# Eight images through masked double attention on one core: row maxima turned by DMA, projections of q and k made whole in every second batch

## What is computed

```
x = x + L(gn(x))                       # x: 8 x 512 x 32 x 32, gn: 32 groups
L(x):
    g    = relu(mean_hw(x) @ w1 + b1) @ w2 + b2
    m    = sigmoid(g) > 0.5            # a gate for each channel
    hyp  = logmap0(mhsa(expmap0(x * m), hdn weights))
    euc  = mhsa(x * (1 - m), eu weights)
    return hyp + euc
mhsa(t):                               # t: 1024 tokens x 512 channels, 8 heads of 64
    q, k, v = split(t @ w_qkv + b_qkv)
    attn = softmax(q @ k.T / sqrt(64)) # 1024 x 1024 for each head
    return (attn @ v) @ w_o + b_o
```

## Time and profile before

| | |
|---|---|
| median of 3 runs | 4022.97 us (4020.16 to 4023.03) |
| the profiled execution's own time | 4021.88 us |
| its span | 4020.2 us |
| TensorE busy | 3937.1 us (98%) |
| GpSimd busy | 2664.2 us (66%) |
| VectorE busy | 2345.5 us (58%) |
| ScalarE busy | 1928.7 us (48%) |

### The profile page before, as it was taken

The page is one execution under the profiler, slowest core; times in us unless marked ns, Lnnn a source line. Parts: engine busy times, 40 slices in busy tenths (PEclk is TensorE's granted clock), DMA queues, the critical chain, the costliest instruction groups (busy, mean ns, idle before and its releaser), DMA issues.

```text
span 4020.2 us, 57048 instructions
## 1 busy us (share of the span) xinstructions
PE 3937.1 (98%) x21664; PEld 2379.5 (59%) x21664; DVE 2345.5 (58%) x2553; ACT 1928.7 (48%) x3489; POOL 2664.2 (66%) x1303
## 2 busy tenths in 40 slices
PE   4999999999999999999999999999999999999998
PEld 3556566565655656556565665656556565565654
DVE  5464755647556475565746557465674656646455
ACT  4454534545345453555535545354553545535443
POOL 4584875838667486674857658675685756858468
PEclk9999999999999999999999999999999999999999
DMA  8212031121311213112141120411113121121101
GB/s 277 100 42 95 32 116 58 43 95 32 124 50 48 95 32 126 53 48 90 32 135 49 48 79 32 142 48 68 53 47 127 48 74 48 56 96 44 58 11 64
DMA packets 137548, 293.12 MB, mean 73 GB/s; under 512 B 16704, under 2 KB 28992, under 8 KB 127296
## 3 DMA queue, kind: packets, MB, share of 16 engines
q1 hardware_dynamic: 137280, 289.47, 21.2%
HBM read 239.09 MB, written 50.33 MB: 72 GB/s over the span
## 4 chain that ended last, share of the span: by engine, by line
PE 94%; DVE 2%; POOL 1%; DMA 1%; issue 1%; ACT 1%; SPq 0%; POOLq 0%; DVEq 0%; ACTq 0%
PE aux_ps L1310 32%; PE acc_ps L1422 23%; PE score_ps L1408 22%; PE aux_ps L1359 8%; PE score_ps L1310 4%; PE aux_ps L1432 3%; DVE mxp L1173 1%; PE aux_ps L1369 1%; POOL sums L673 1%; DMA w_split<-v_y 0%; DMA w_split<-w_o 0%; DMA xin<-in_x_dram 0%; PE aux_ps L1328 0%; PE aux_ps L1325 0%; POOL w_o L653 0%
## 5 line engine op out<-in xcount | busy, mean ns | idle before, releaser
L673 POOL TENSOR_TENSOR sums<-sums,probs 128x1024 f32<-128x1024 f32 x768 | 1835.4, 2390 | 736.9 <-ACT probs L850 682.6
L1173 DVE TENSOR_REDUCE mxp<-aux_ps 128x2 f32<-128x1024 f32 x1014 | 1241.7, 1225 | 1299.9 <-PE aux_ps L1359 1291.5
L850 ACT ACTIVATE probs<-score_ps 128x512 f32<-128x512 f32 x2048 | 1058.1, 602 | 658.7 <-PE score_ps L1408 648.0
L1422 PE MATMUL acc_ps<-probs,v_y 128*64 128x512 f32 x4096 | 991.9, 605 | 0.0
L1310 PE MATMUL aux_ps<-xs,w_qk 128*128 128x512 f32 x2976 | 804.7, 408 | 0.0
L1310 PEld LDWEIGHTS aux_ps<-xs,w_qk 128*128 128x128 f32 x2976 | 524.8, 188 | 374.3 <-issue 279.1
L673 POOL TENSOR_TENSOR sums<-probs 128x1024 f32<-128x1024 f32 x128 | 305.0, 2383 | 432.8 <-ACT probs L850 432.1
L1422 PEld LDWEIGHTS acc_ps<-probs,v_y 128*64 128x64 f32 x4096 | 248.2, 136 | 475.2 <-issue 245.2
L1359 PE MATMUL aux_ps<-k_hi,q_hi 64*128 64x512 f32 x2028 | 454.0, 443 | 18.7 <-DVE mxp L1173 16.1
L1235 DVE RECIPROCAL den<-den 128x256 f32<-128x256 f32 (+1 forms) x240 | 443.4, 1848 | 17.3 <-ACT den L861 17.3
L1408 PE MATMUL score_ps<-q_hi,k_hi 64*128 64x512 f32 x2048 | 407.9, 393 | 1.0 <-issue 1.0
(11 more groups left out here) (142 smaller groups left out, 3195.2 us busy)
## 6 DMA issues: line engine op xcount, KB each, us to landing
w_qk<-w_split SPq DMA_DIRECT2D x124, 512.0 KB, 4.2
xin<-in_x_dram SPq DMA_DIRECT2D x232, 256.0 KB, 3.3
w_o<-w_split SPq DMA_DIRECT2D x32, 1024.0 KB, 7.3
w_v<-w_split SPq DMA_DIRECT2D x30, 1024.0 KB, 5.9
v_y<-in_x_dram SPq DMA_DIRECT2D x72, 256.0 KB, 3.0
y<-v_y SPq DMA_DIRECT2D x64, 256.0 KB, 2.0
xin<-y SPq DMA_DIRECT2D x64, 256.0 KB, 2.9
out_dram<-v_y SPq DMA_DIRECT2D x64, 256.0 KB, 6.5
```

Of the source, the lines that this page charges most:

```text
L673: pool.tensor_tensor(sums[h][:, :], a, probs[:, g % SLOTS_P, :], ALU.add).then_inc(c_sum[h].sem, 1)
L850: act.activation(probs[:, n % SLOTS_P, token_half(u % 2)], score_ps[:, u % SCORE_BANKS, :], ACT.Exp, scale=SCALE).then_inc(c_exp.sem, 1)
L1173: dve.tensor_reduce(mxp[:, :, n, h], ps, AX.X, ALU.max).then_inc(c_free["D"].sem, 1)
L1422: last = nc.tensor.matmul(acc_ps[head(j), :], v_y[:, m, head(2 * p + j)], probs[:, n % SLOTS_P, token_half(j)], start=(m == 0), stop=(m == ...
```

## The change

Row maxima. `combine` runs twice for each pair, after slots 11 and 15, once for each half of the queries. SyncE stores each result to DRAM (1024 numbers of 4 bytes, one by one) and, once this has landed, loads it back as two rows into `q_max` (`load_neg`). The matmuls, the identity and the copies are gone. The score tile waits for the load at the first tile of each phase.

Projections. Each stands whole in one batch, which is always even. The denominators move from `b` = 4`ph` + 5 to 4`ph` + 6 (even), for the last phase but one to 28, and the reciprocal comes in one piece at 4`ph` + 8 (30 for that phase).

Chains. The gate's third and fourth tile move from batches 10 and 12 to 12 and 14. Most of VectorE's small steps of the second half now stand in odd batches.

```diff
-GATE_BATCH = {4: "mean", 6: "var", 10: "hidden", 12: "gate"}
+GATE_BATCH = {4: "mean", 6: "var", 12: "hidden", 14: "gate"}
-CLAMP, POWER, ROOT, NORM, EXP, INVERT, SCALES, BLEND = 6, 6, (7, 8), 8, 8, 9, 10, 11
-SERIES = {6: (0, 1), 9: (2,), 10: (3, 4)}
+CLAMP, POWER, ROOT, NORM, EXP, INVERT, SCALES, BLEND = 5, 5, {7: (0, 1), 9: (2,)}, 9, 9, 10, 11, {11: (0, 1), 13: (2,)}
+SERIES = {5: (0,), 6: (1,), 8: (2,), 9: (3,), 10: (4,)}
-SCALE_AT, SCALE_TAIL = {12: (0,), 14: (1, 2), 18: (4,), 19: (5,), 22: (7,)}, {15: (3,), 21: (6,)}
+SCALE_AT, SCALE_TAIL = {13: (0,), 15: (3,), 19: (5,), 21: (6,)}, {14: (1, 2), 18: (4,), 22: (7,)}
-Y_SERIES = {5: (0,), 26: (1, 2, 3), 27: (4,)}
-Y_BLEND = 30
+Y_SERIES = {23: (0, 1), 25: (2, 3, 4)}
+Y_BLEND = 27
-DRAIN, DEN, MULT, SPLIT, LOW = 4, 5, 9, 10, 12
-RECIP, RECIP_PARTS = [6, 8], 4
+DRAIN, MULT, SPLIT, LOW = 4, 9, 10, 12
+DEN, RECIP, RECIP_PARTS = 6, 8, 4
...
-            done = min(8 * p + QK_AT[k], BATCHES)
-            first = done if (p, k) in ((PAIRS, 0), (PAIRS + 1, 3)) else done - 1
-            out += [("qk", p, k, part) for part in range(2) if b == (first, done)[part]]
+        out += [("qk", p, k) for k in range(4) if b == min(8 * p + QK_AT[k], BATCHES)]
...
+            def load_neg(i, t, p, h):
+                n = 0 if i is None else 4 * t + p
+                sp.wait_ge(c_mx.sem, c_mx.at(i, h + 1 if i is None else 2 * (n - 1) + h + 1))
+                if i is not None:
+                    sp.wait_ge(c_neg[h].sem, c_neg[h].at(i, 16 * (n - 1)))
+                sp.dma_start(max_dram[h].rearrange("j (n q) -> q (j n)", q=P),
+                             mxw[:, h, :, :].bitcast(F32).rearrange("p j n -> p (j n)")).then_inc(c_mst[h].sem, 16)
+                sp.wait_ge(c_mst[h].sem, c_mst[h].at(i, 16 if i is None else 16 * n))
+                last = TILES * t + 16 * (p - 2) + 8 * h + 8
+                if i is not None and (i or last > 0):
+                    sp.wait_ge(c_score.sem, c_score.at(i, 2 * last))
+                sp.dma_start(q_max[0:HD + 1:HD, p % 2, token_half(h)].bitcast(F32), max_dram[h]).then_inc(c_neg[h].sem, 16)
...
-            def combine(i, t, p):
-                aux_read(dve, i, (t, "max", p, 15))
-                for j in range(2):
-                    dve.tensor_reduce(mxw[:, HD * j:HD * j + NT], mxp[:, j, :, :], AX.X, ALU.max,
-                                      negate=True).then_inc(c_mx.sem, 1)
+            def combine(i, t, p, h):
+                aux_read(dve, i, (t, "max", p, HALF_DONE[h]))
+                if i is not None:
+                    dve.wait_ge(c_mst[h].sem, c_mst[h].at(i, 16 * (4 * t + p - 1)))
+                dve.tensor_reduce(mxw[:, h, :, :], mxp[:, :, 4 * h:4 * h + 4, :], AX.X, ALU.max,
+                                  negate=True).then_inc(c_mx.sem, 1)
...
-            def neg_rows(i, t, p):
-                pe.wait_ge(c_mx.sem, c_mx.at(i, 2 if t < 0 else 2 * (4 * t + p)))
-                for h in range(2):
-                    ps = bank_free(pe, i, (t, "neg", p, h))
-                    for n in range(4):
-
-                        last = nc.tensor.matmul(ps[0:HD + 1, n * P:(n + 1) * P], mxw[:, 4 * h + n:4 * h + n + HD + 1],
-                                                ident[:, :], start=True, stop=True)
-                    last.then_inc(c_aux.sem, 1)
...
+                        if m == 0:
+                            pe.wait_ge(c_neg[h].sem, c_neg[h].at(i, 16 * (4 * t + p)))
```

151 lines of the change are left out of this document (70 added, 81 removed).

## The result

The changed kernel takes 4139.78 us (median of 5 runs, 4134.53 to 4144.06) against 4022.24 us (median of 5, 4020.16 to 4023.03): a ratio of 1.0291, 95% interval 1.0277 to 1.0306. It is slower by 117.5 us, outside the range of the prediction and on the other side of its two likeliest cases. The span of the profiled execution is 4132.8 us, 112.6 more than before.

The account below looks back on a forecast made before the run. TensorE, busy 3937.1 of 4020.2 us, was taken as the bound. A gain of 73 us against 75 us of waits gave 4025 us; the likeliest case spanned 4001 to 4046, the 8-in-10 range 3966 to 4072.

Parts of the forecast that it names:

- its two likeliest cases: Whole kernel: gain and waits about equal, 4001 to 4046 us, chance 0.45; short batches hold, 3950 to 4001, chance 0.33.
- the first end: Row maxima's DMA store: lands after about 4 us, nearest row 3.7; at the other end 13.0 in a full queue.
- the range of pair 2: First halves, pair 2: SyncE has 7 us for 7 to 8.5 us of work; 0.5 us, 8 times, 4 us.
- The third rival: Score tiles: maxima come late if store and load exceed 15 us or SyncE is held; 4046 to 4110 us, chance 0.08.
- The start: Before the first score tile: the first store stands behind split weights in a full queue; 3 us, 0 to 8.
- 30 + 40: TensorE's gain: 30 us from no longer turning maxima in the loop, 40 us from 202 merged pairs of half projections.
- the ledger: VectorE in short batches of second halves: 0.65 us free in 4.37; waits of 5.15 us, 36 us in 7 images.
- the second rival: Second halves: VectorE steps after GpSimd's start wait up to 2.4 us; 4053 to 4081 us, chance 0.14.
- the sign of being right: TensorE's waits on the maxima sum to 50 to 60 us, mostly before even batches' first maxima slots in second halves.
- 1.0 + 0.95 + 0.9: First halves' waits: 1.0 us for tiny VectorE steps, 0.95 in batch 28, 0.9 before batch 24's projection.
- The first rival: Odd batches stay at 4.37 us without waits, or a third to two thirds of them; 3950 to 4001 us, chance 0.33.
- the forecast's near balance of gains and waits: Whole kernel: 75 us of waits against 73 us of gain, giving 4025 us; 4001 to 4046, chance 0.45.

Follow-up runs that it names:

- runs16: Changed kernel with the row maxima stored in 16-byte runs instead of 4-byte pieces, the adding matmul reading them with a stride: 4190.53 us.
- fetch4: Changed kernel with the store writing 32 bytes of each partition in one run and the fetch picking 4-byte elements: 4054.64 us, a single run.
- pair2: Changed kernel with SyncE's store of pair 2's first maxima, in first halves, ahead of the second masked chunk's load: 4054.42 us.
- maxima_by_dma: Kernel before with only the row maxima by DMA instead of TensorE, projections, denominators and chains as before: 4030.21 us.
- cured: Changed kernel with 32-byte stores, a fetch of 4-byte elements, and pair 2's first store ahead of the second masked chunk: 4046.76 us.
- fetch4_before: Kernel before with the row maxima by DMA, stores of 32 bytes a partition and a fetch picking 4-byte elements: 4014.18 us.

## Why the prediction was wrong

**The step that failed** is the row maxima's landing: "I take the first end, since the queue is nearly idle in the loop". The first end was 4 us, from a load of 4-byte pieces; a store of twice as many took 10.5. That stays under the 13.0 of the earlier trace rows, which was the other end, but I didn't carry it through: the range of pair 2 ("from 0 to 3 each") didn't use it. By the prediction's own arithmetic, 7 us were left for store and fetch; 10.5 and, on average, 3.4 us for the way back need 7 more. TensorE waited 8.0, and the low clock behind the wait made of it the 10.3 that batches 15 and 16 lost. The price stood at 4 us for the kernel, and is 72. The 3 us for the way back were right. The occupation of the queue (22.5% of the engines' time) said nothing about it, because an in-order wait isn't occupation. `runs16`, `fetch4` and `pair2` show the cause from two sides: shorten the landing or put other work into it, and batches 15 and 16 lose 8 to 10 us of their 10.3 in each of seven images.

**The third rival** named the mechanism ("SyncE comes to them behind a wait") and priced it up to 4110, with a chance of 0.08. It priced it as 3 us at every pair; it was 10.3 us at one pair in eight, in seven images, where the prediction had already counted only 7 us for the work. That place should have had the greatest weight.

**What SyncE is kept from** was left out. The prediction priced the wait of the score tile, and never what stands behind L548 in SyncE's program. At the start of an image the last half's maxima stand ahead of the output stores and the next chunks: batch 2 lost 2.9 us in images 2 to 7 and 7.7 in the first. `maxima_by_dma` lost 1.5 there in images 2 to 7, and `fetch4` nothing.

**The clock** had no term: a wait was priced by its length alone. Behind each wait of batch 16 the granted clock was 0.50 and the batch 2.1 us longer; in `cured` it costs some 11 us behind the waits of batch 21.

**The start**: 3 us predicted (0 to 8), 13 measured, and 2.6 more in the first image's first half. The first store landed after 19.6 us behind the split weights in the queue. Even 32-byte pieces took 14 there, so most of it is the queue's, not the pieces'.

**The gain** came short but near. Turning by DMA gave 1.4 us per second half and 1.9 per first half (`fetch4_before` against before, the last image's late stretch aside), some 25 us of the 30. The merged projections show their size in batches 8 to 11 of the second halves: 24.33 us without waits against 24.68, 0.35 for two pairs where 0.2 each stood. By these two the whole gain is some 60 us, an estimate (25 and 202 times 0.175), where 30 + 40 stood.

**The waits of the second halves** were predicted by the ledger as 5.15 us and measured as 6.2 on the same batches. All but one of its terms are within 0.7 us: batch 7 0.5 (0.6), 11 0.3 (0.3), 13 0.4 (1.1), 15 0.4 (0.7), 19 0.2 more than before (0.1), 23 to 27 1.1 (1.0). Batch 21 was 3.1 (0.9): the second rival, which said that a step would be late there "by tenths of a us only". It was late by 0.20, and that was enough. In batch 21 the scaling stands ahead of the low part and the second maximum, so its 1.6 extra us are all TensorE's. Over the kernel TensorE waited 74.4 us for the maxima before a maxima slot, where 50 to 60 were named as the sign of being right. Batches 6 and 10 at 0.35 us each, which I hadn't, batches 24 and 28 (0.5 together, 0.9 predicted) and the 0.75 that batch 19 already waited before make up the rest of the 8.2.

**The first halves' own waits** (batches 12, 24 and 28: 0.6, 0.6 and 0.7 us, gate tiles apart) came where predicted but for batch 12: 1.9 us where 1.0 + 0.95 + 0.9 stood. In batch 12 the trace names the wait, the gate's third tile waits until VectorE has read a maximum out of the bank that it goes to:

```profile
1728.07 1.05 PE L1337 MATMUL aux_ps<-small,xin 128*128 128x1 f32 x8 [0.51 <-DVE mxp L1182]
```

They eat most of what merging gives: cured first halves take 244.8 us with whole projections, 244.9 with halves.

So on the way from 4139.8 to 4022: 85 to 93 us go with the landing's wait, by the cures one at a time or together, the difference of the two landings included; 27 us remain in `cured` (span 4046.8), 10 of them the start, 33 the second halves (some 11 by the clock), less 16 that the first halves and the last half of all have gained. The first rival ("the short batches hold") and the forecast's near balance of gains and waits both fell short in the second halves even without the store.

## What to carry to other kernels

Price a DMA between two engines as issue, landing and fetch, and then read the program of the engine that waits for the landing: what is behind that wait pays as well, and a wait that is there anyway (a gate tile here) is where the landing is free. When a transfer has to change the order of elements, put the small pieces on the read from DRAM rather than on the write: here the store fell from 10.5 to 1.4 us and the way back rose by 1.5. Before shortening a batch, list the two-input steps of VectorE that it holds: one that comes after GpSimd's start can cost the rest of the GpSimd instruction (2 us here), and moving it may only pick the next one. And read the granted clock behind each long wait of TensorE; a wait can cost more than its length.
